# Silu by one table function, forget gate by tanh with a GpSimd step, and a new order of calls in a fused attention and FFN kernel

## The reference

```python
# layer 1: gated linear recurrence
q = silu(x @ Wq1 @ Wq2)                  # 512 wide
f = sigmoid(x @ Wk1 @ Wk2)
a = exp(log_sigmoid(f)); k = 1 - a       # so a = sigmoid(sigmoid(z))
h[t] = a[t] * h[t-1] + k[t] * v[t]       # v = x @ Wv, a scan over the tokens
out = rmsnorm(q * h) * norm_w @ Wo
# layer 2: six blocks, layernorm with gain and bias between them
x = gelu(x @ w1.T + b1) @ w2.T + b2 + x
```

## Time and profile before

| what | us |
|---|---|
| median of 3 runs | 629.62 |
| lowest and highest | 629.15, 630.03 |
| the profiled execution | 629.86 |
| its span in the trace | 628.0 |

### The profile page before, as it was taken

How to read it: one execution, slowest core, us unless ns; L and a number is a source line. 1 busy time by engine, 2 the same in 40 slices (tenths; PEclk the granted TensorE clock), 3 DMA queues, 4 the chain that set the end, 5 groups by cost and what they waited for, 6 DMA issues and landing times.

```text
span 628.0 us, 8878 instructions
## 1 busy us (share of the span) xinstructions
PE 619.8 (99%) x2893; PEld 516.4 (82%) x2893; DVE 470.1 (75%) x820; ACT 407.9 (65%) x688; POOL 250.4 (40%) x232
## 2 busy tenths in 40 slices
...
DMA packets 56877, 25.13 MB, mean 40 GB/s; under 512 B 47360, under 2 KB 52864, under 8 KB 56832
## 3 DMA queue, kind: packets, MB, share of 16 engines
...
...
## 4 chain that ended last, share of the span: by engine, by line
PE 92%; DVE 3%; issue 2%; ACT 2%; POOL 1%; POOLq 0%; DVEq 0%; ACTq 0%
PE BK L169 47%; PE BK L351 38%; PE BK L301 3%; PE BK L175 1%; PE BK L366 1%; PE BK L198 1%; DVE OL L534 1%; PE BK L242 0%; POOL X L1188 0%; ACT R L835 0%; PE BK L262 0%; PE BK L253 0%; PE BK L254 0%; PE BK L232 0%; ACT R L849 0%
## 5 line engine op out<-in xcount | busy, mean ns | idle before, releaser
L945 ACT ACTIVATE HH<-BK,B 128x512 fp32r<-128x512 f32 x192 | 132.1, 688 | 140.5 <-PE BK L169 136.2
L563 DVE TENSOR_TENSOR HL<-BK,HH 128x512 fp32r<-128x512 f32 x192 | 130.7, 683 | 83.3 <-ACT BK L951 82.8
L169 PE MATMUL BK<-XH,WL 128*128 128x512 f32 x416 | 162.5, 391 | 0.7 <-DVE HL L563 0.7
L169 PE MATMUL BK<-XL,WH 128*128 128x512 f32 x416 | 162.1, 390 | 0.0
L169 PE MATMUL BK<-XH,WH 128*128 128x512 f32 x416 | 162.0, 389 | 0.0
L351 PE MATMUL BK<-HH,WL 128*128 128x512 f32 x368 | 143.7, 390 | 0.0
L351 PE MATMUL BK<-HH,WH 128*128 128x512 f32 x368 | 143.2, 389 | 0.0
L351 PE MATMUL BK<-HL,WH 128*128 128x512 f32 x368 | 143.2, 389 | 0.0
L951 ACT ACTIVATE BK<-BK,B 128x512 f32<-128x512 f32 x192 | 125.8, 655 | 0.0
L169 PEld LDWEIGHTS BK<-XH,WL 128*128 128x128 f32 x416 | 78.1, 188 | 17.3 <-DVE HL L563 1.1
L169 PEld LDWEIGHTS BK<-XH,WH 128*128 128x128 f32 x416 | 78.1, 188 | 16.5
(11 more groups left out here) (149 smaller groups left out, 793.8 us busy)
## 6 DMA issues: line engine op xcount, KB each, us to landing
...
G<-sums SPq DMA_DIRECT2D x160, 8.0 KB, 1.8
...
sums<-P SPq DMA_DIRECT2D x40, 8.0 KB, 1.4
...
```

The lines of the kernel that those rows point to most:

```text
L169: r = eng.matmul(dst, s, m, start=i == 0, stop=i == len(todo) - 1)
L563: eng.tensor_tensor(HL[:, g % HR, :], bank["mm1", n, j][:, :], HH[:, g % HR, :].bitcast(f32), ALU.subtract).then_inc(S["hlo"], 1)
L945: eng.activation(HH[:, g % HR, :], bank["mm1", n, j][:, :], ACT.Gelu, bias=B1[:, 8 * (n // 4) + j:8 * (n // 4) + j + 1]).then_inc(S["ghi"], 1)
```

## The change

Tiles 0 and 1 (`SILU = 2`) now take silu in one ACT instruction, read from `zq` in PSUM, and DVE's `q` is gone for them. Their gate is made by the two tanh steps in all tiles, and a new POOL step `decay` makes a = t2/2 + 1/2 for tiles 0 and 1; tiles 2 and 3 keep ACT's `a`. The function that warms up the activation table is Silu and no longer Sigmoid. Four constants share one semaphore. The lists of calls of all five engines are new from the start to the entry of the loops, and again after the loops; the loops are unchanged.

```diff
+SILU = 2
@@ tensor
-                freed[b] = S["q"], 4 * t + m + 1
+                freed[b] = (S["silu"], 4 * t + m + 1) if t < SILU else (S["q"], 4 * (t - SILU) + m + 1)
@@ tensor, order (the start)
-            zq(0, 2, 0); zk(0, 0, 1); v(0, 0, 2); zk(0, 1, 3); v(0, 1, 4); zk(0, 2, 5); zq(0, 3, 1); v(0, 2, 0)
-            zk(0, 3, 3); v(0, 3, 2); proj(0, 0); turn1(1, 0, 5); turn1(1, 1, 3); proj(0, 1); up(1, 0, 1); up(1, 1, 4)
+            zk(0, 0, 1); zq(0, 2, 0); zk(0, 1, 3); v(0, 0, 2); zk(0, 2, 5); v(0, 1, 4); zq(0, 3, 1); zk(0, 3, 3)
+            v(0, 2, 0); v(0, 3, 2); turn1(1, 0, 5); turn1(1, 1, 3); proj(0, 0); up(1, 0, 1); up(1, 1, 4); u(1, 0)
+            u(1, 1); proj(0, 1); zq(1, 0, 0); zq(1, 1, 5); zk(1, 0, 3); v(1, 0, 1); zq(1, 2, 2); zk(1, 1, 3)
...
@@ tensor, order (third tile's last transposes)
-            mm1(1, 6, 3); proj(3, 3); mm2(1, 3); rms(3, 2); mm1(1, 7, 0); mm2(1, 4); mm2(1, 5); mm2(1, 6)
-            mm1(2, 0, 1); mm2(1, 7); mm1(2, 1, 2); mm1(2, 2, 3); mm2(2, 0); mm1(2, 3, 0); turn3(3, 0, 1)
+            turn3(2, 1, 0); proj(3, 3); mm1(1, 5, 1); mm1(1, 6, 3); rms(3, 2); mm2(1, 4); mm1(1, 7, 0); mm1(2, 0, 1)
+            mm1(2, 1, 2); mm2(1, 5); mm1(2, 2, 3); mm2(1, 6); mm2(1, 7); mm1(2, 3, 0); mm2(2, 0); mm1(2, 4, 3)
+            mm2(2, 1); turn3(3, 0, 1); turn3(3, 1, 2); mm2(2, 2); mm2(2, 3); mm1(2, 5, 1); mm1(2, 6, 2); mm1(2, 7, 0)
@@ vector
             def kv(t, m):
...
+                ve.wait_ge(S["t2"], 4 * t + m + 1)
+                eng.scalar_tensor_tensor(vb[:, :], KB[:, p, :], -1.0, vb[:, :], ALU.add, ALU.mult).then_inc(S["kv"], 1)
             def scan(t, m):
...
+                if t < SILU:
+                    ve.wait_ge(S["decay"], 4 * t + m + 1)
@@ vector, order (the end)
+            z_mv(21, 1); hlo(23, 2); y(22, 0); z_nm(21, 1); y(22, 1); swap(2, 0); z_mv(21, 2); swap(2, 1); hlo(23, 3)
+            hlo(23, 4); z_mv(21, 3); z_nm(21, 2); z_nm(21, 3); hlo(23, 5); fin0(1, 2); z_st(22, 0); z_st(22, 1)
+            z_st(22, 2); z_mv(22, 0); z_mv(22, 1); z_mv(22, 2); hlo(23, 6); z_st(22, 3); z_mv(22, 3); hlo(23, 7)
@@ scalar
-                eng.activation(WARM[:, :], ONE[:, :], ACT.Sigmoid)
+                eng.activation(WARM[:, :], ONE[:, :], ACT.Silu)
+            def silu(t, m):
+                i = 4 * t + m
+                ac.wait_ge(S["zq"], i + 1)
+                gate_free(i)
+                eng.activation(QB[:, m, :], bank["zq", t, m][:, :], ACT.Silu).then_inc(S["silu"], 1)
             def t1(t, m):
...
-                if t < 2:
-                    eng.activation(FB[:, :], bank["zk", t, m][:, :], ACT.Sigmoid).then_inc(S["t1"], 1)
-                else:
-                    eng.activation(FB[:, :], bank["zk", t, m][:, :], ACT.Tanh, scale=0.5).then_inc(S["t1"], 1)
+                eng.activation(FB[:, :], bank["zk", t, m][:, :], ACT.Tanh, scale=0.5).then_inc(S["t1"], 1)
@@ scalar, order (the start)
+            wv_hi(); uhi(0, 1); silu(0, 0); silu(0, 1); t1(0, 0); t2(0, 0); wp_hi(1); t1(0, 1); wo_hi(); t2(0, 1)
+            silu(0, 2); t1(0, 2); ohi(0, 0); t2(0, 2); l1_nm(1, 0); l1_nm(1, 1); l1_nm(1, 2); l1_nm(1, 3); t1(0, 3)
+            xhi1(1, 0); silu(0, 3); xhi1(1, 1); t2(0, 3); ohi(0, 1); osq(0, 0); wp_hi(2); uhi(1, 0); osq(0, 1)
@@ scalar, order (the end)
+            gf(22, 7); ghi(23, 0); gf(23, 0); ghi(23, 1); gf(23, 1); pre(0); pre(1); pre(2); ghi(23, 2); gf(23, 2)
+            ghi(23, 3); pre(3); gf(23, 3); away2_1(0); away2_1(1); away2_1(2); away2_1(3); ghi(23, 4); gf(23, 4)
+            ghi(23, 5); gf(23, 5); ghi(23, 6); gf(23, 6); z_ng(2, 0); z_ng(2, 1); z_ng(2, 2); ghi(23, 7); gf(23, 7)
@@ gpsimd
+            def decay(t, m):
+                i, p = 4 * t + m, m % 2
+                po.wait_ge(S["t2"], i + 1)
+                if i >= 2:
+                    po.wait_ge(S["scan"], i - 1)
+                eng.tensor_scalar(AB[:, p, :], KB[:, p, :], 0.5, 0.5, ALU.mult, ALU.add).then_inc(S["decay"], 1)
@@ gpsimd, order (the start)
+            nw_minus(); wv_lo(); wo_scaled(); decay(0, 0); l1_ve(1); l1_ng(1); l1_rs(1); l1_nb(1); wo_lo()
+            decay(0, 1); decay(0, 2); wp_lo(1, 0); wp_lo(1, 1); decay(0, 3); wp_lo(2, 0); ssum(0, 1); wp_lo(2, 1)
@@ sync, order (the end)
-            away(0, 0); away(0, 1); tokens(0, 0); stored(0, 0); stored(0, 1); stored(0, 2); stored(0, 3); away(1, 0)
-            away(1, 1); tokens(1, 1); away(3, 0); away(3, 1); stored(1, 0); tokens(3, 3); stored(1, 1); stored(1, 2)
+            away(0, 0); away(0, 1); tokens(0, 0); away(1, 0); away(1, 1); tokens(1, 1); stored(0, 0); away(3, 0)
+            away(3, 1); tokens(3, 3); stored(0, 1); away(2, 0); stored(0, 2); stored(0, 3); stored(1, 0)
```

More of the change, by code:

```diff
@@ L26 @@
 ldb1 ldb2 ldlg ldlb ldp0 ldp1 put1 got1 put2 got2 away0 away1 away2_0 away2_1 away3 half_tokens tokens0 tokens1
-tokens2 tokens_last stored one mhalf quarter half eps idle_in nw sel wq1_hi wk1_hi wq2_hi wk2_hi wv_hi wo_hi wq1_lo
+tokens2 tokens_last stored one consts idle_in nw sel wq1_hi wk1_hi wq2_hi wk2_hi wv_hi wo_hi wq1_lo
 wk1_lo wq2_lo wk2_lo wv_lo wo_lo wo_scaled bias wp_hi wp_lo f_st f_mv f_ve f_rs f_nm l1_st l1_mv l1_ve l1_ng l1_rs
 l1_nb l1_nm l2_st l2_mv l2_ve l2_ng l2_rs l2_nb l2_nm x1 l3_st l3_mv l3_ve l3_ng l3_rs l3_nb l3_nm turn1 turn3
-xhi1 xlo1 xhi3 xn xlo3 xhi xlo up u uhi ulo zq tq q zk t1 t2 a v kv scan o ohi osq olo proj ssum sq_turn sq_part
+xhi1 xlo1 xhi3 xn xlo3 xhi xlo u uhi ulo zq tq q silu zk t1 t2 decay a v kv scan o ohi osq olo proj ssum sq_turn sq_part
 rms ms mm1 ghi gf hlo mm2 y sum1 tr1 red1 tot1 mub ctr sqr sum2 tr2 red2 tot2 vae rsd rsb nn res swap swap_last pre
@@ new lines, in _ @@
+            v(2, 1, 4); zk(2, 1, 3); proj(1, 3); mm1(0, 0, 1); mm1(0, 1, 2); rms(1, 3); mm1(0, 2, 0); zq(2, 3, 3)
+            mm1(0, 3, 1); mm1(0, 4, 2); mm2(0, 0); mm2(0, 1); zk(2, 2, 0); mm2(0, 2); proj(2, 0); mm1(0, 5, 3)
+            proj(2, 1); turn3(1, 0, 1); turn3(1, 1, 2); v(2, 2, 0); mm2(0, 3); mm1(0, 6, 1); turn1(3, 0, 2)
+            turn1(3, 1, 3); mm2(0, 4); up(3, 0, 2); up(3, 1, 0); mm1(0, 7, 3); u(3, 0); zk(2, 3, 1); u(3, 1)
+            proj(2, 2); zq(3, 0, 1); zq(3, 1, 2); v(2, 3, 3); zq(3, 2, 0); zk(3, 0, 1); v(3, 0, 2); mm2(0, 5)
```

287 lines of the change are left out of this document (133 added, 154 removed).

## The result

The changed kernel takes 630.78 us (median of 16 runs, 630.03 to 631.23), the kernel before 629.23 (16 runs, 628.32 to 630.03). The ratio is 1.0025, 95% interval [1.0018, 1.0032]: 1.5 us slower, where 1.3 faster was forecast. The profiled execution took 631.03 us, with a span of 629.2 (before: 629.86 and 628.0). The mean granted clock is 0.999 and was 0.998.

What follows compares the result with a forecast made beforehand. PE, busy 99% of the span, was taken as the bound, with 2.1 us of its waits to be had. Terms -1.0 - 0.7 + 0.2 + 0.3 = -1.2, taken as -1.3, gave a 628.3 us median; range 627.0 to 630.6.

Steps and rivals of the forecast that it cites:

- silu and tanh in different tables: Rival, chance 0.04: ACT reloads its table at each of eleven changes between Silu and tanh; 638 us.
- the `decay` is dear: Rival, chance 0.05: each decay on POOL takes 3.0 us, so PE waits at up(1, 1); 631.3 us.
- Contention: POOL's decay locking out DVE's olo, eight times at most; 0.2 us in PE for all new small waits.
- (a): PE's wait at tile 1's transposes turn1(1), 25.02 us; 0.5 us, to shrink to about 0.1.
- (d): PE's wait at turn3(3), 148.56 us, for ACT's last l3_nm; 0.7 us, to go wholly.
- (b): PE's wait for olo at the proj starting at 30.85 us; 0.5 us with restart, to go.
- (c): PE's wait ahead of zq(1, 0), 32.66 us; 0.4 us with restart, to go.
- 0.2 were set aside: Allowance of 0.2 us in PE for all new small waits, from decay holding back one or two olo.
- the lead is lost again: Rival, chance 0.28: new waits in the body as large as the old; 629.6 us, from 629.0 to 630.3.
- The end, +0.3: Term for the new order behind the loops: 0.3 us lost, through ghi(23, 7), the last hlo and fin0.
- the end: Rival, chance 0.13: transfers of tiles 3 and 2 land a us later, ACT and gelu wait; 630.3 us.
- one of my signs of being wrong: Listed sign that the forecast fails: pre or z_st(22) end PE's work late by over a us.

Runs made afterwards that it cites:

- e2: The kernel before with only the call lists behind the loops (all engines but PE) in the new order; 631.28 us, ratio 1.0044 to before.
- e1: The changed kernel with the call lists behind the loops (all engines but PE) taken back to the old order; 628.69 us, ratio 0.9995 to before.
- e5: The changed kernel with three stores of finished blocks moved behind half_tokens on SyncE's queue; 629.70 us, ratio 1.0016 to before.
- e13: e6 with GpSimd's powers of tile 2 in a row (z_rs(22, 2) ahead of z_ve(22, 3), fin1(1, 3) last); 629.68 us, ratio 1.0009 to before.
- e17: e13 with the three stores ahead of the turned half tile and GpSimd's fin1(1, 3) ahead of the powers; 629.17 us, ratio 1.0007 to before.
- e6: The changed kernel with the three stores behind half_tokens and ACT's pre behind gf(23, 2); 629.62 us, ratio 1.0010 to before.
- e3: The changed kernel with tile 2's statistics behind hlo(23, 6) and z_ng behind ghi(23, 7) again; 630.93 us, ratio 1.0040 to before.
- e7: e1 with each of the eight decay steps on GpSimd done twice; 629.64 us, ratio 1.0008 to before.
- e8: e1 with l1_nm ahead of t2(0, 2) on ACT, scan(0, 1) and o(0, 1) ahead of kv(0, 2) on DVE; 628.61 us, ratio 0.9996 to before.
- e14: e1 with ACT's weight step wp_hi(1) moved from ahead of t1(0, 1) to behind l1_nm(1, 3); 628.71 us, ratio 0.9993 to before.

## Why the prediction was wrong

It was a range from 627.0 to 630.6 with 0.16 on slower. Point by point:

- **Prices.** Silu 0.590 for 0.6, `decay` 0.721 for 0.9 in bounds of 0.53 and 1.30, `t2` 0.729 for 0.728, one load ahead of Gelu. The rivals *silu and tanh in different tables* and *the `decay` is dear* are out. The load ahead of Gelu took 1.283 us, and between Silu and Tanh there is none. The Trainium skill ("ScalarE: Activation LUTs", What ACT_TABLE_LOAD costs) gives about 1283 ns for a load; the trace agrees.
- **Contention.** Forecast: up to eight more `olo` held back. Measured: their excess fell from 4.3 us to 16 x (0.714 - 0.68) = 0.5. The long one of the earlier trace rows is gone: the longest `olo` is 0.91 now, where three took 1.71 to 1.80. I had priced only the new `decay`, and not what the new order did to the rest: in the changed trace `ssum` and `wp_lo` hardly fall on an `olo` any more. No run shows what that was worth in time.
- **The body, (a) to (d).** (b), (c) and (d) went as forecast. (a) did not: `l1_nm` was due at 23.7 and came at 24.0, while PE, which had started 0.3 us earlier, got there at 23.3; 0.8 us of gap instead of 0.1. The term that I had put at nothing is ACT's wait for the weights of `wp_hi(1)`, 1.10 us in this trace. With 0.35 at 114.97, where 0.2 were set aside, the body's sum was -1.0 - 0.7 + 0.2 = -1.5. The traces give, from 584.0 (mean of before and e2) to 583.2 (mean of nine with the new body, 582.4 to 583.6): -0.8. The times give -0.4 to -0.65. So the rival *the lead is lost again* describes the body about half: 0.7 to 1.1 us of the 1.5 was not there.
- **The end, +0.3.** This is the step that failed. It measured +1.9 by the times (changed less e1; +2.2 for e2 less before) and +2.3 to +2.5 by the traces. The rival *the end*, held at 0.13, names what happened: transfers land later than I had them, with ACT and the gelu behind them; its price of 2 us is near as well. I give the two places in us behind the last tile's first `mm1`, 596.47 in the earlier trace rows and 595.17 in the changed kernel.
  - *Tile 3.* I let its tokens go at 598.4, 1.9 behind; they go 2.7 behind, and 3.1 in e2. My figure fits the old place of `swap_last`: there SP's issues of `away(3)` end level with the `mm1` and need some 2 us to land. In the new list of DVE the first `swap_last` starts 4.2 us ahead of the `mm1`, where it was 15.7, and the issues end 1.1 behind. I had counted the one wait less on SP, and not the later turn on DVE. So the three `pre` run from 6.8 to 7.8 where the gelu is free at 7.1 (603.61 - 596.47), and it starts 0.6 late. In e2 it starts 1.0 late.
  - *Tile 2.* I had `ghi(23, 7)` at 618.1, 21.6 behind; it runs at 618.76, 23.6 behind, since the statistics that `z_ng` needs wait for the last half tile. PE's last matmul starts 28.8 behind, 26.6 in the kernel before. That is one of my signs of being wrong: `z_st(22)` ends PE's work late by over a us.

  By the clock of the span the first place does not look late: `pre` was forecast at 602.7 to 603.7 and ran at 602.00 to 603.0. That is only because PE was 1.3 us earlier in the new trace. The lead itself did no harm. e1 has it, and there the transfers came along to a tenth; e2 has little of it (a body of 583.8 us), and loses as much.
- **What I had costed at nothing.** "SP's other moves have no one waiting": three stores beside the last turn held `half_tokens` and so `z_st(22)` back, 0.9 us (e5). The powers of tile 2 were spread, 0.6 us on DVE (e13), and GpSimd's `fin1(1, 3)` behind them held nine stores until 622 us, which took 0.4 of that back until e17; with both put right the end fell by another 0.7 in the trace (e6 32.6, e17 31.9) and 0.3 in time, where the intervals overlap. With `pre` (0.1 by the time, 0.5 by the trace) they make up e17, whose end is nearly that of before. e3's part, the gelu behind `z_ng`, is worth nothing while the transfer is late.

Two things stay open. One is whether e17 is really slower than e1: by the differences to before it stands 0.7 us above, with intervals that overlap, though its end is within 0.2 in the trace, but the execution in that trace was the fastest of its eleven. The other is the price of `decay` beyond its length (e7). No kernel run here beats both clearly: e1, e8 and e14, the new body with the old end, lie 0.3 to 0.4 us below before, within what these runs can tell from nothing.
